# A transformer layer with attention and 32 experts: a beginning with six tiles ahead and joined DMAs, and the first experts' rows gathered at the end of routing

## The reference

```python
q, k, v = (split_heads(x @ w.T) for w in (wq, wk, wv))      # 4 heads of 64; q and k scaled
q, k = rope(q), rope(k)
attn = softmax(q @ k.T + causal_mask)                       # per sequence and head
x = layernorm(x + (attn @ v).reshape(B, T, D) @ wo.T)
# router: 6 statistics per token, a hidden layer of 128 with gelu, 32 experts, the best two
h = gelu(concat(x, stats(x)) @ r1_w.T + r1_b)
probs = softmax(h @ r2_w.T)
topp, topi = top_k(probs, 2)
idx = the 320 tokens of highest probability of each expert   # cap = 1.25 * 8192 / 32
ye = (silu(gate(x[idx])) * up(x[idx])) @ w_down             # per expert
out = scatter_add(w * ye) + 0.05 * adapters of 16 groups
x = layernorm(x + out)
```

## Time and profile before

| | us |
|---|---|
| median of three runs | 2142.7 (2142.36 to 2144.84) |
| the profiled execution | 2145.87 |
| its span, first to last instruction | 2144.1 |
| attention | 0 to about 1332 |
| routing | 1335 to 1571 |
| experts | 1571 to about 2091 |
| last normalisation | to 2144 |
| PE busy, share of the span | 1853.9, 86% |
| DVE busy | 1308.9, 61% |
| ACT busy | 975.8, 46% |
| POOL busy | 798.0, 37% |

### The profile page before, as it was taken

One profiled execution on the slowest core, in us unless ns is written; L12 is line 12 of the kernel. 1 busy time (PEld: TensorE's weight loads), 2 busy tenths in 40 slices (PEclk: granted clock), 3 DMA queues, 4 the chain that ended last, 5 costly groups with the idle time before them and its releaser, 6 DMA issues. The chain is left out here.

```text
span 2144.1 us, 38575 instructions
## 1 busy us (share of the span) xinstructions
PE 1853.9 (86%) x12834; PEld 1660.0 (77%) x12834; DVE 1308.9 (61%) x2935; ACT 975.8 (46%) x2165; POOL 798.0 (37%) x983
## 2 busy tenths in 40 slices
PE   5899999999999999999999995521669999999980
PEld 4688888888888888888888884511669999999980
DVE  5466654577663677663667743677856565666645
ACT  2244344344343444444443442243546666666646
POOL 3242043431142431243431101000656666766643
PEclk9799999999999999999999997555789999999995
DMA  4443134333234432234432211300024444544419
GB/s 113 113 105 99 53 99 110 99 103 95 65 96 111 105 103 81 73 92 116 102 96 78 69 50 47 136 0 0 1 79 134 152 144 156 152 154 144 147 32 313
DMA packets 189208, 215.24 MB, mean 100 GB/s; under 512 B 26672, under 2 KB 154664, under 8 KB 184964
## 3 DMA queue, kind: packets, MB, share of 16 engines
q1 hardware_dynamic: 173188, 203.12, 31.3%
q0 software_dynamic: 15872, 10.24, 2.9%
HBM read 129.66 MB, written 56.62 MB: 87 GB/s over the span
## 5 line engine op out<-in xcount | busy, mean ns | idle before, releaser
L572 PEld LDWEIGHTS out_ps<-v_sb,probs 128*128 128x128 f32 x4352 | 565.3, 193 | 20.8
L572 PE MATMUL out_ps<-v_sb,probs 128*128 128x65 f32 x4352 | 573.9, 271 | 0.0
L784 DVE TENSOR_REDUCE part_max<-rows_ps 128x1 f32<-128x512 f32 (+2 forms) x576 | 346.6, 618 | 183.3 <-PE rows_ps L531 113.2
L686 ACT ACTIVATE probs<-scores_ps 128x512 f32<-128x512 f32 (+3 forms) x640 | 329.4, 537 | 152.4 <-PE scores_ps L559 76.6
L1566 PE MATMUL up_ps<-xe_t,w 128*128 128x320 f32 x1920 | 289.7, 311 | 1.7 <-DVE xe_t L1673 1.7
L1566 PEld LDWEIGHTS up_ps<-xe_t,w 128*128 128x128 f32 x1920 | 284.6, 189 | 2.2 <-issue 1.9
L555 PE MATMUL scores_ps<-q,k_st 128*128 128x512 f32 (+2 forms) x640 | 272.9, 426 | 2.8 <-ACT probs L686 1.3
L528 PE MATMUL rows_ps<-k_st,q 128*128 128x512 f32 (+3 forms) x640 | 249.5, 404 | 22.2 <-DMA q<-q_low_cols 10.3
L960 POOL TENSOR_TENSOR products<-qk,cos_sin 128x256 f32<-128x256 f32 x236 | 169.5, 751 | 241.8 <-ACT qk L653 241.8
L556 PE MATMUL scores_ps<-q,k 68*128 68x512 f32 (+2 forms) x640 | 236.0, 369 | 0.0
L1529 POOL DMA_INDIRECT acc_rows<-out_rows,token x96 | 148.7, 1549 | 128.7 <-ACT out_rows L1656 117.4
(11 more groups left out here) (276 smaller groups left out, 2731.5 us busy)
## 6 DMA issues: line engine op xcount, KB each, us to landing
w_raw<-in_w_expert SPq DMA_DIRECT2D x32, 1536.0 KB, 6.3
k<-k_st SPq DMA_DIRECT2D x160, 128.0 KB, 2.3
k_st<-parts SPq DMA_DIRECT2D x128, 128.0 KB, 2.4
q<-q_up_cols SPq DMA_DIRECT2D x128, 128.0 KB, 2.8
w_raw<-in_w_adapter SPq DMA_DIRECT2D x32, 384.0 KB, 6.9
x_t<-in_x_t SPq DMA_DIRECT2D x64, 128.0 KB, 2.3
q_up_cols<-parts SPq DMA_DIRECT2D x64, 128.0 KB, 2.4
q_low_cols<-parts SPq DMA_DIRECT2D x64, 128.0 KB, 2.4
```

The lines of the kernel that those rows point to most:

```text
L572: mm = pe.matmul(o_ps[:, u % 2, s * (HD + 1):(s + 1) * (HD + 1)], probs[:, g % P_RING, s * P:(s + 1) * P], v_sb[:, place(b, j), h, :], sta ...
L686: act.activation(probs[:, g % P_RING, low:CH], s_ps[:, g % S_RING, low:CH], ACT.Exp).then_inc(exp_done, 1)
L784: red = dve.tensor_reduce(to, r_ps[:, e % R_RING, 0:width], AX.X, ALU.max, negate=g == 0)
```

## The change

There are three parts.

1. **Six tiles ahead.** FIRST goes from 8 to 6. All ropes of these six tiles are on DVE, and POOL only splits inputs; the splits of the other weights (`w_o`, `w_r1`, `w_r1s`) move ahead of the first rope. The inputs of eight tiles (FIRST_X) are still loaded and split ahead. Tiles 6 and 7 are projected and turned in the stream from slots 0 and 2, tiles 8 to 15 some slots later than before, and the maxima of unit 4 move from slots 1 to 8 into slots 8 to 12. `load_q` of units 0 to 3 stands between the stores of tiles 3, 4 and 5.
2. **Joined DMAs.** The two tables of q halves become one, and both halves of a tile are stored by one DMA. `q1` is loaded by one DMA whose source is named twice (`to_broadcast([2, HD, CH])`) in place of two DMAs.
3. **Gathers in routing.** `rows` and its semaphores are made outside of the two blocks. POOL clears `rows` early in routing, and behind its last `lane_hot` it gathers the rows of experts 0 and 1 by `slot_token` itself; `experts` starts with expert 2's gather.

```diff
-FIRST = 8
-FIRST_ON_POOL = (1, 4, 7)
+FIRST = 6
+FIRST_X = FIRST + 2
...
-            at = (0, 0, 0, 0, 2, 2, 3, 3, 5, 5, 6, 6)[n - GROUP] if e[0] == "max" else (1, 4, 8)[u - 1]
+    first_pieces = ((0, 0, 0, 0), (2, 2, 3, 3), (5, 5, 6, 6), (8, 9, 9, 10, 10, 11, 11, 12))
+    first_turns = (1, 4, 8, 13)
...
-        if b == 0:
-            project_at[n] = 9 * (t - FIRST) // 2 if t < 12 else 20 + 9 * (t - 12)
+        if n < FIRST_X:
+            project_at[n] = 2 * (t - FIRST)
+        elif b == 0:
+            project_at[n] = 4 + 9 * (t - 8) // 2 if t < 12 else 22 + 9 * (t - 12)
...
-                for part_, to in enumerate(("q_up", "q_low")):
-                    sp.dma_start(dram[to][:, :, n * P:(n + 1) * P].rearrange("h d t -> d h t"),
-                                 raw(parts[0:HD, n % 2, part_])).then_inc(qk_stored[n % 2], 16)
+                sp.dma_start(dram["q"][:, :, :, n * P:(n + 1) * P].rearrange("a h d t -> d a h t"),
+                             raw(parts[0:HD, n % 2])).then_inc(qk_stored[n % 2], 16)
...
-                for to in (q1[0:HD, r], q1[HD:P, r]):
-                    sp.dma_start(raw(to), dram["q_up"][h, :, tokens]).then_inc(q_loaded[r], 16)
-                sp.dma_start(raw(q2[0:HD, r]), dram["q_low"][h, :, tokens]).then_inc(q_loaded[r], 16)
+                sp.dma_start(raw(q1[:, r]), dram["q"][0, h, :, tokens].unsqueeze(0).to_broadcast([2, HD, CH]))\
+                  .then_inc(q_loaded[r], 16)
+                sp.dma_start(raw(q2[0:HD, r]), dram["q"][1, h, :, tokens]).then_inc(q_loaded[r], 16)
...
-            for n in range(2, FIRST + 2):
+            for n in range(2, FIRST_X):
                 load_xt(n)
-                if n >= 4:
-                    store_qk(n - 4)
+                if n >= 5:
+                    store_qk(n - 5)
             for u in range(HEADS):
+                if FIRST_X - 5 + u < FIRST:
+                    store_qk(FIRST_X - 5 + u)
                 load_q(u)
                 load_k2(u)
-                if u < 2:
-                    store_qk(FIRST - 2 + u)
...
             rope(0)
             for n in range(FIRST):
-                if n + 1 < FIRST and n + 1 not in FIRST_ON_POOL:
+                if n + 1 < FIRST:
                     rope(n + 1)
                 lower(r_ps[:, n % 2, :], n)
...
+            wait(pool, rows_cleared, 1, pool_passed)
+            wait(pool, tokens_listed, 1, pool_passed)
+            for e in range(2):
+                for t in range(SL):
+                    n = min(P, cap - t * P)
+                    pool.indirect_dma_start(
+                        out=rows[0:n, e, t, :], out_offset=None, in_=dram["x1"],
+                        in_offset=bass.IndirectOffsetOnAxis(ap=slot_token[0:n, e, t:t + 1], axis=0),
+                        bounds_check=NTT * P - 1, oob_is_err=False).then_inc(gathered[e], 16)
...
-            for r in range(2):
-                gather(r, r, False)
```

More of the change, by code:

```diff
@@ L101, in attention_plan @@
         begins[u] = max(slot, -1)
[L102 to L110, removed]
-            at = (0, 0, 0, 0, 2, 2, 3, 3, 5, 5, 6, 6)[n - GROUP] if e[0] == "max" else (1, 4, 8)[u - 1]
+    first_pieces = ((0, 0, 0, 0), (2, 2, 3, 3), (5, 5, 6, 6), (8, 9, 9, 10, 10, 11, 11, 12))
+    first_turns = (1, 4, 8, 13)
+    before = [*pieces_of(0), ("turn", 0)]
+    stream = [[e for e in now if e[1] > HEADS] for now in stream]
+    assert not stream.pop(0)
+    for u, (slots, turn) in enumerate(zip(first_pieces, first_turns), 1):
+        for e, at in zip(pieces_of(u), slots, strict=True):
             stream[at].append(e)
-            begins[u] = min(begins[u], at)
+        stream[turn].append(("turn", u))
+        begins[u] = slots[0]
     for now in stream:
@@ L133, in attention_plan @@
         finish_at.append(at)
-    chains = [(project_at[n], n, (("xt", 0, False), ("proj", 3, True), ("rope", 0, False), ("v", 1, True),
-                                  ("turn", 3, True)))
-              for n in range(FIRST, COUNT)]
+    chains = []
+    for n in range(FIRST, COUNT):
+        load = (("xt", 0, False), ("proj", 3, True)) if n >= FIRST_X else (("proj", 0, True),)
+        chains.append((project_at[n], n, load + (("rope", 0, False), ("v", 1, True), ("turn", 3, True))))
     for i in range(COUNT):
@@ L141, in attention_plan @@
         chains.append((finish_at[i], i, steps + ((("hidden", 2, True),) if i % 2 else ())))
-    after = {"proj": ("rope", 1), "ot": ("wo", AT_RING), "wo": ("x1", ROW_RING), "x1": ("x1t", ROW_RING),
+    after = {"xt": ("v", 2), "proj": ("rope", 1), "ot": ("wo", AT_RING), "wo": ("x1", ROW_RING), "x1": ("x1t", ROW_RING),
              "x1t": ("hidden", 1)}
@@ L428, in _ @@
                 turned = made.get(("turn", b * NT + GROUP * g + GROUP - 1), -2)
-                assert turned + 3 < begins[u] or u < 2 * HEADS
+                assert turned + 2 < begins[u] or u <= HEADS
                 if u >= HEADS:
@@ L900, in lower_xt @@
                     .then_inc(xt_split, 1)
[L902 to L914, removed]
-            pool.wait_ge(weights_loaded, 16 * 6)
[L916 to L919, removed]
-                    sums_of(n - 2)
-            for n in FIRST_ON_POOL:
-                if n + 2 >= FIRST:
-                    products_of(n)
-                    sums_of(n)
+            for n in range(FIRST_X):
+                lower_xt(n)
+            pool.wait_ge(weights_loaded, 16 * 6)
             def main(g):
@@ L1420, in load_weights, with experts @@
     sp.dma_start(w_raw[:, r, UP + DOWN:], dram["w_adapter"][group]).then_inc(w_loaded[r], 16)
-def experts(nc, dram, T, cap, slot_token, slot_weight, w_raw, w_loaded):
+def experts(nc, dram, T, cap, slot_token, slot_weight, w_raw, w_loaded, rows, gathered):
     SL = slot_token.shape[2]
@@ L1461, in experts @@
         listed_in = sem("listed_in")
-        gathered = [sem(f"gathered{r}") for r in range(2)]
         scattered = sem("scattered")
@@ L1798, in build @@
     dram["hidden"] = nc.dram_tensor("hidden_cols", (HID, T), F32).ap()
-    for name in ("q_up", "q_low"):
-        dram[name] = nc.dram_tensor(f"{name}_cols", (HEADS, HD, T), F32).ap()
+    dram["q"] = nc.dram_tensor("q_cols", (2, HEADS, HD, T), F32).ap()
     with ExitStack() as ctx:
@@ L1806, in build @@
         w_raw = ctx.enter_context(nc.sbuf_tensor("w_raw", [P, 2, W], F32))
-        route(nc, dram, NTT, cap, slot_token, slot_weight, w_raw, w_loaded)
-        experts(nc, dram, T, cap, slot_token, slot_weight, w_raw, w_loaded)
+        rows = ctx.enter_context(nc.sbuf_tensor("rows", [P, 2, SL, D], F32))
+        gathered = [ctx.enter_context(nc.semaphore(f"gathered{r}")) for r in range(2)]
+        route(nc, dram, NTT, cap, slot_token, slot_weight, w_raw, w_loaded, rows, gathered)
+        experts(nc, dram, T, cap, slot_token, slot_weight, w_raw, w_loaded, rows, gathered)
     last_norm(nc, dram["acc"], out, NTT)
```

59 lines of the change are left out of this document (32 added, 27 removed).

## The result

| | median us | range | ratio to before |
|---|---|---|---|
| before | 2143.4 | 2142.4 to 2144.8 | |
| after | 2206.1 | 2203.9 to 2210.9 | 1.0297 [1.0283, 1.0311] |
| predicted | 2148 | 2124 to 2164 | |

A forecast was written before the change was run, and what follows sets the result against it. It took PE to bound attention and the experts, with the beginning held by a loop through SP. Terms 3.5 + 3 - 6.0 - 1.5 - 5 = -6.0, applied to the 2142.7 median, gave 2148.7, stated as 2148, range 2124 to 2164.

The forecast's parts named there:

- The joined load: Load of q1 with a twofold outer dimension: runs on two engines, landing in 7.7 to 8.9 us, 7.7 taken.
- The start of the stream: Beginning of attention up to unit 5's first row: earlier q, less the wait at unit 4, gains 3.5 us.
- Unit 8: Slots 28 to 32, after tile 11's later turning: PE waits 6.0 us for q, and lower clock costs 1.5.
- The other units: Later loads of q, ordered five slots ahead: short leads are exceeded, costing 5 us in all, bounds 0 and 25.
- The gathers: End of routing: the first expert's products start 3 us earlier, at 1585.1, then held by the weight splits.
- (a): Rival for the joined load: spread over engines like the others, landing in 2.8; 17.2 us faster, 2126; chance 0.27.
- (c): Rival: two engines at 18.9 KB/us, the stream waits 25 us, the start gains nothing; 2168 to 2172; chance 0.13.
- The signs it named: Trace checks: landing of q 2.8 or near 8, first maxima near 41, waits at units 4, 5, 8, products' start.

The follow-up runs named there:

- e1: The changed kernel with q1 loaded again by two DMAs of 64 rows each, from the joined table: 2138.1 us, ratio 0.9984 to before.
- e12: The kernel of e1 measured once more, beside three other kernels on one chip: 2142.3 us, ratio 0.9989 to before.
- e11: The kernel of e1 with a tile's q stored by two DMAs into the joined table in place of one: 2143.2 us, ratio 0.9986 to before.
- e6: The kernel of e1 with tiles 8 to 11 projected 4 slots apart and unit 4's maxima in slots 10 to 12: 2138.5 us, ratio 0.9978 to before.

## Why the prediction was wrong, point by point

- **The joined load.** The mechanism was the one forecast: two engines. The rate was about right too (25 KB/us against 22.9), and the landing of 9.5 was 1.8 above the 7.7 taken, and 0.6 above its bound. At 25 KB/us an engine's 128 KB take about 5.2 us (an estimate), so some 4.3 us of the 9.5 are not transfer, where the prediction took 2. The Trainium skill ("DMA: Bandwidth & Descriptors", the part on 16 increments) puts the count at the largest number up to 16 that divides the outermost sizes of both sides. The traces here agree: 2 outermost, 0.13 of 16 engines; 64 or 128 outermost, loads of q in 2.8 to 3.1 us.
- **The start of the stream, +3.5.** First row 44.0 for 40.8, unit 4's 86.8 for 81.4, unit 5's 92.8 for 87.2. Unit 0's 3.2 are 1.4 from the store (q asked for at 34.4; landing 3.3, not 2.4) and 1.8 from the landing. Unit 4's 5.4 are these, carried on to turn 7 (71.7 for 68.7), 0.8 more on the way from that turning to the order, and 1.6 from its own landing (77.54 to 86.79). The term became -4.4, counted up to unit 8's wait.
- **Unit 8, -6.0 and -1.5.** The wait was 8.9 by the same landing, the clock after it 7.2. The place was right; the wait was too small by 2.9 and the clock behind it by 5.7.
- **The other units, -5: the step that failed.** It measured 42.4, and its outer bound was 25. These 37 us are two thirds of the 55 by which the four terms missed. Its mechanism was there: PE waits for q three or four times in each later sequence, at most 2.0 us each, 12.8 in all where 5 were taken. What it put at nothing is the clock behind these waits, the other 30 us: PE's busy time for the same work is 31.3 us longer, and after a wait of 1.87 us PE works at the half level for 20. The text had charged the clock at the start (2.5) and for unit 8 (1.5) and nowhere else, though the profile before shows the half level behind the gaps of the beginning. No run filled the later waits to keep the clock up; that it is the clock rests on the traces. The queue of four short units in a row, which made its bound of 25, did form (units 19 to 21 begin 20 to 27 us after their load's issue, where before had 10 to 20), but none of them made PE wait.
- **The gathers, +3.** The move turned one stall into another as forecast: 2.0 in the trace, 2 to 3 by the medians. The first gather starts 1.0 us after the list and the block ends 1.6 us behind the last: that is the difference.
- **Rivals.** (a), 2126, would have been wrong as well: with a fast load the rest of the change gives 2138 to 2142. Its 16 us for the beginning counted the arrival at slot 8 (27.6 us earlier in e1) and unit 4's wait, but by slot 27 10 are left and by slot 59 some 2, as more tiles are still to be made in the stream and the waits at units 4 and 8 each cost clock. (c), two engines and a stream that waits 25 us, put its point of decision at "a landing above some 9 us", and the landing was above it, but it too had the loss as waiting and none as clock: 2172 where 2206 was measured.
- **The signs it named.** They said that a landing near 8 and a time under 2138 would show wrong leads; they had no line for a time far above, because nothing in the text multiplied a wait by the clock. (The sum's 2148.7 rounds to 2149, not 2148, which changes nothing.)

## What to carry to other kernels

Before two DMAs are joined into one, look at the outermost count of the joined access pattern on both sides: if it falls from 64 to 2, as here, the bytes go by two engines, 25 KB/us each, and the engine that issues the next ones is held. A short wait of PE in a saturated stream is to be priced with the clock behind it. Here three waits of 1.6 to 2.0 us were followed by 16 to 20 us at half speed each, so eight to ten lost, and two of 1.7 and 1.8 by 3 and 7: the length of the wait alone did not tell. Over the whole stretch 11 us of added idle time came with 31 of slower work. A beginning that arrives earlier with less work done is worth what is left at a slot where both have done the same.

## What was not expected of the hardware

- SP is held when it issues behind a slow DMA: 2.9 to 5.6 us for an issue that otherwise takes 0.5, eleven times; what stands behind in its list is issued later too.
- One program takes 2133 to 2151 us in 22 runs (e1 and e12), and a wait of 3 us on PE is followed by the half level for 3 us in one of its traces and 20 in the other. The eleven runs of e11 fall into two groups, four at 2135 to 2137 and seven at 2143 to 2144.
- Products that nobody reads, put in PE's waits, raise the mean granted clock between 35 and 57 us from 0.61 (e6) to 0.77. That they also steady the times is not shown: they span 4 and 8 us in two sets of runs, and the unfilled e6 spans 8.
